# One-core Trainium2 kernel of four image stages: rows of q and k written by SBUF transfers, the neighbour mask as extra contraction rows, channel products on GpSimd, a new order of steps

## What is computed

```
stage 0: x1 = x + gap(x) . (w_conv x) . softmax_j(x^T x)
stage 1: q, k (16 rows each) and v (128 rows) are 1x1 projections of x1 with batch norm folded in
         x2 = x1 + gamma * v . softmax_j(q^T k)^T
stage 2: a, s (16 rows each) = relu(projection of x2)
         h_s = softmax over the 8 neighbours of a pixel of a^T s, applied to x2
         h_p = softmax over the 2 neighbouring channels of x2 x2^T, applied to x2
         x3 = (1 - gama) x2 + gama * elu(h_s + h_p)
stage 3: a 2-D Fourier transform of 16 projections of x3, gains by direction, inverse, added to x3
```

## Time and profile before

| | us |
|---|---|
| median of 3 runs (lowest, highest) | 290.1 (289.94, 290.49) |
| the profiled execution: its own time | 290.33 |
| the profiled execution: span in the trace | 288.5 |
| mean granted TensorE clock | 0.991 of full speed |
| instructions in the trace | 4440 |

### The profile page before, as it was taken

The page is one execution under the profiler, slowest core; times in us unless marked ns, Lnnn a source line. Parts: engine busy times, 40 slices in busy tenths (PEclk is TensorE's granted clock), DMA queues, the critical chain, the costliest instruction groups (busy, mean ns, idle before and its releaser), DMA issues.

```text
span 288.5 us, 4440 instructions
## 1 busy us (share of the span) xinstructions
PE 272.3 (94%) x1499; PEld 178.6 (62%) x1499; DVE 213.2 (74%) x325; ACT 186.2 (65%) x355; POOL 95.1 (33%) x102
## 2 busy tenths in 40 slices
PE   7999999999999899999999999799999799999994
PEld 3846555467677576747657464467867557765462
DVE  3865889789998786763489867799788775828383
ACT  0774676789997474766648776688748457674320
POOL 1045031505236878128004101354279814000000
PEclk9999999999999999999999999979999999999998
DMA  6951000000000000000000000000000000000015
GB/s 184 353 202 51 0 1 1 2 0 1 3 0 1 0 2 0 1 3 0 0 3 1 0 2 1 1 0 2 1 0 2 1 0 3 2 4 0 2 73 220
DMA packets 4520, 8.14 MB, mean 28 GB/s; under 512 B 1118, under 2 KB 2014, under 8 KB 4498
## 3 DMA queue, kind: packets, MB, share of 16 engines
q1 hardware_dynamic: 4498, 7.85, 7.8%
HBM read 5.68 MB, written 2.10 MB: 27 GB/s over the span
## 4 chain that ended last, share of the span: by engine, by line
PE 66%; DVE 10%; POOL 8%; ACT 8%; issue 3%; DMA 2%; SPq 1%; DVEq 0%; POOLq 0%; ACTq 0%
PE psum L360 64%; POOL e1h L1047 4%; ACT e L686 3%; DVE e1l L900 3%; DMA qs<-row 2%; ACT psum L677 2%; POOL ks L1040 1%; DVE nmax L884 1%; POOL qs L1037 1%; SPq L348 1%; DVE nmax L850 1%; ACT qs L669 1%; POOL regionb L1010 1%; ACT ks L670 1%; DVE x L860 1%
## 5 line engine op out<-in xcount | busy, mean ns | idle before, releaser
L1047 POOL CAST e1h<-e 128x1024 fp32r<-128x1024 f32 x32 | 42.6, 1333 | 34.7 <-ACT e L686 21.6
L900 DVE TENSOR_TENSOR e1l<-e,e1h 128x1024 fp32r<-128x1024 f32 x32 | 40.8, 1282 | 9.8 <-POOL e1h L1047 9.7
L686 ACT ACTIVATE e<-psum 128x1024 f32<-128x1024 f32 x32 | 32.8, 1025 | 20.6 <-DVE e1l L900 15.7
L850 DVE TENSOR_REDUCE nmax<-psum 128x1 f32<-128x1024 f32 x32 | 39.0, 1221 | 9.3 <-PE psum L360 8.7
L657 ACT ACTIVATE e<-psum,nmax 128x1024 f32<-128x1024 f32 x32 | 35.7, 1115 | 14.2 <-issue 9.6
L884 DVE TENSOR_REDUCE nmax<-psum 128x1 f32<-128x1024 f32 x32 | 38.0, 1217 | 3.9 <-PE psum L360 3.8
L677 ACT ACTIVATE psum<-psum,nmax 128x1024 f32<-128x1024 f32 x32 | 34.8, 1089 | 7.0 <-DVE nmax L884 6.3
L360 PE MATMUL psum<-e,v0n 128*64 128x512 f32 x128 | 31.0, 604 | 0.0
L360 PE MATMUL psum<-ks,qs 96*128 96x512 f32 (+2 forms) x96 | 30.1, 405 | 0.8 <-DVE ks L874 0.4
L360 PE MATMUL psum<-qs,ks 96*128 96x512 f32 (+2 forms) x96 | 28.9, 389 | 1.8 <-DMA qs<-row 1.3
L360 PE MATMUL psum<-xh 128*128 128x512 f32 x64 | 28.3, 442 | 0.6 <-DVE x L860 0.3
(11 more groups left out here) (175 smaller groups left out, 491.4 us busy)
## 6 DMA issues: line engine op xcount, KB each, us to landing
out<-xin SPq DMA_DIRECT2D x8, 256.0 KB, 2.1
xin<-in_x SPq DMA_DIRECT2D x3, 512.0 KB, 6.1
twist<-in_twist_in SPq DMA_DIRECT2D x1, 768.0 KB, 7.4
zz<-in_region_in SPq DMA_DIRECT2D x2, 360.0 KB, 3.5
xin<-in_x SPq DMA_DIRECT2D x2, 256.0 KB, 2.8
untwist<-in_untwist_in SPq DMA_DIRECT2D x1, 512.0 KB, 7.2
zz<-in_near_in SPq DMA_DIRECT2D x1, 288.0 KB, 4.4
rw<-in_rows_w SPq DMA_DIRECT2D x1, 256.0 KB, 2.7
```

The source lines that it names most:

```text
L686: inc(go(e1[:, E1_AT[b, i], :], t[:, :], ACT.Exp), "e1_ready", b)
L850: inc(vec.tensor_reduce(nmax0[z][:, i:i + 1], t[:, :], AX.X, ALU.max, negate=True), "nmax0_ready", b)
L900: inc(vec.tensor_tensor(e1l[:, EH_AT[b, i], :], e1[:, E1_AT[b, i], :], e1h[:, EH_AT[b, i], :].bitcast(F32), ALU.subtract), "e1l_ready", b)
L1047: done(gp.tensor_copy(e1h[:, EH_AT[b, i], :], e1[:, E1_AT[b, i], :]), "e1h_ready", b, i)
```

## The change

The parts of the diff that matter:

- **Rows.** qs and ks now have 80 rows and a margin of 32 pixels on either side. Groups are of 17 rows (16 and one for the shift). ACT writes the high parts of a projection in one activation of 128 x 512 to a buffer hi, DVE the rests in one to a buffer lo. SP then issues 12 transfers from SBUF to SBUF of 17 rows x 2 KB each: 8 from hi, 4 from lo. score and near wait for all 12. The steps qkdup and asdup of POOL are gone. SP has a written list of its own.
- **Bias.** For q and k the bias goes in with ACT and DVE; the pair of bias matmuls stays for a and s only.
- **Mask.** The neighbour mask is 29 further contraction rows of qs and ks, written once by four transfers of 29 rows x 4.3 KB after a cast on POOL. A window is one matmul with 80 rows and 192 columns. The mask's load stands behind those of images 2 and 3.
- **Channels.** chan's 8 matmuls and its mask become a product of neighbouring channels on POOL (cprod, 128 x 1016) and three sums (csum), then three fp32 matmuls of one or two columns. ecn is built from two columns by three DVE instructions in place of one.
- **Start.** POOL's memsets are others and more, and eight small copies clear the margins. The fold step has one transpose fewer.
- **Order.** All step lists are rewritten. On PE between a projection and the first matmul that reads its rows (or the shift rows that SP issues behind them) stand now: image 0 qk: gram, gap, gram, mix; image 1 qk: gram, shift1, val1; image 2 qk: gram, mix, chanT, gram, half of nearT, gram, gram; image 3 qk: shift1, val1, scoreT, scoreT; image 0 as: attH, scoreT, attL three times; image 1 as: xconv, chanT, x2T, half of nearT, mix; image 2 as: attL, scoreT, x2T, attH, scoreT, attL, attH, attL; image 3 as: shift2, chan, xturn, x2T, chanT, nearT.

```diff
 G = 32
+R = HID + 1
-KS3 = 3 * G
+KS3 = 3 * R
+MASKS = 29
+KS4 = KS3 + MASKS
...
-    "normv.0.0 masks.0.0 normv.0.1 normv.0.2 regions.0.0 split.1.0 split2.1.0 normv.0.3 normv.1.0 qkdup.0.0 "
-    "qkdup.0.1 normv.1.1 normv.1.2 normv.1.3 split.2.0 split2.2.0 qkdup.1.0 qkdup.1.1 e1h.0.0 e1h.0.1 e1h.0.2 "
-    "e1h.0.3 e1h.0.4 e1h.0.5 e1h.0.6 e1h.0.7 regions.0.1 e1h.1.0 e1h.1.1 e1h.1.2 normv.2.0 e1h.1.3 e1h.1.4 "
-    "asdup.0.0 e1h.1.5 asdup.0.1 e1h.1.6 e1h.1.7 normv.2.1 asdup.1.0 normv.2.2 asdup.1.1 split.3.0 xkeep.0.0 "
-    "normv.2.3 split2.3.0 qkdup.2.0 normv.3.0 qkdup.2.1 normv.3.1 normv.3.2 normv.3.3 xkeep.1.0 qkdup.3.0 "
-    "qkdup.3.1 e1h.2.0 e1h.2.1 e1h.2.2 e1h.2.3 e1h.2.4 e1h.2.5 e1h.2.6 e1h.2.7 e1h.3.0 e1h.3.1 e1h.3.2 xkeep.2.0 "
-    "e1h.3.3 e1h.3.4 asdup.2.0 asdup.2.1 e1h.3.5 e1h.3.6 e1h.3.7 asdup.3.0 asdup.3.1 xkeep.3.0")
-
-SP_STEPS = [(name, b, int(name == "shift2")) for name, b, i in DVE_STEPS if name in ("shift1", "shift2")]
+    "nears.0.0 normv.0.0 normv.0.1 split.1.0 split2.1.0 normv.0.2 normv.0.3 regions.0.0 normv.1.0 regions.0.1 "
+    "normv.1.1 normv.1.2 split.2.0 split2.2.0 normv.1.3 e1h.0.0 e1h.0.1 e1h.0.2 e1h.0.3 e1h.0.4 e1h.0.5 normv.2.0 "
+    "e1h.0.6 e1h.0.7 e1h.1.0 e1h.1.1 e1h.1.2 e1h.1.3 e1h.1.4 e1h.1.5 e1h.1.6 cprod.0.0 e1h.1.7 normv.2.1 csum.0.0 "
+    "split.3.0 split2.3.0 normv.2.2 cprod.1.0 normv.2.3 xkeep.1.0 xkeep.0.0 csum.1.0 normv.3.0 normv.3.1 "
+    "normv.3.2 normv.3.3 e1h.2.0 e1h.2.1 e1h.2.2 e1h.2.3 e1h.2.4 e1h.2.5 e1h.2.6 e1h.3.0 e1h.3.1 e1h.2.7 e1h.3.2 "
+    "e1h.3.3 e1h.3.4 e1h.3.5 e1h.3.6 e1h.3.7 cprod.2.0 csum.2.0 xkeep.3.0 cprod.3.0 csum.3.0 xkeep.2.0")
+
+SP_STEPS = steps(
+    "regin.0.0 nearin.0.0 regin.0.1 qkhi.0.0 qklo.0.0 qkhi.1.0 qklo.1.0 row1.0.0 row1.1.0 ashi.0.0 aslo.0.0 "
+    "row2.0.0 ashi.1.0 aslo.1.0 row2.1.0 qklo.2.0 qkhi.2.0 row1.2.0 qkhi.3.0 qklo.3.0 row1.3.0 ashi.2.0 aslo.2.0 "
+    "row2.2.0 ashi.3.0 aslo.3.0 row2.3.0")
...
+        qs = two("qs", [KS4, NW], F32R)
+        ks = two("ks", [KS4, NW], F32R)
+        hi = two("hi", [P, HALF], F32R)
+        lo = two("lo", [P, HALF], F32R)
...
+            sp.dma_start(near, near_in).then_inc(const_in, 16)
...
+            def rows(dst, at, src, k, z):
+
+                for h in range(2):
+                    o = h * 2 * G + k * G
+                    sp.dma_start(dst[z][at * R:(at + 1) * R, W + h * HALF:W + (h + 1) * HALF].bitcast(F32),
+                                 src[z][o:o + R, :].bitcast(F32)).then_inc(s["qk_in"][z], 16)
+
+            for name, b, i in SP_STEPS:
                 z = b % 2
-                wait(sp, "row_ready", b, n)
-                for k, to in ((0, HID), (1, 2 * G + HID)):
-                    sp.dma_start(qs[z][to:to + 1, :].bitcast(F32).rearrange("o (u p) -> o u p", p=P),
-                                 row[z][k * CH:(k + 1) * CH, :].bitcast(F32)).then_inc(s["shift_in"][z], 16)
+                if name in ("row1", "row2"):
+                    wait(sp, "row_ready", b, int(name == "row2"))
+                    for k, to in ((0, HID), (1, 2 * R + HID)):
+                        sp.dma_start(qs[z][to:to + 1, W:W + N].bitcast(F32).rearrange("o (u p) -> o u p", p=P),
+                                     row[z][k * CH:(k + 1) * CH, :].bitcast(F32)).then_inc(s["shift_in"][z], 16)
+                elif name == "nearin":
+                    wait(sp, "nearr_ready", 0)
+                    for k in range(2):
+                        for n, dst in enumerate((qs, ks)):
+                            sp.dma_start(dst[k][KS3:KS4, :].bitcast(F32),
+                                         nearr[n * 32:n * 32 + MASKS, :].bitcast(F32)).then_inc(near_sem, 16)
+                elif name == "regin":
+                    if i:
+                        wait(sp, "regions_ready", 0)
+                    sp.dma_start(region, region_in[:, i]).then_inc(region_sem, 16)
+                elif name in ("qkhi", "ashi"):
+                    wait(sp, "hi_ready", b, int(name == "ashi"))
+                    for dst, at, k in ((qs, 0, 0), (ks, 0, 1), (qs, 1, 0), (ks, 2, 1)):
+                        rows(dst, at, hi, k, z)
+                elif name in ("qklo", "aslo"):
+                    wait(sp, "low_ready", b, int(name == "aslo"))
+                    for dst, at, k in ((qs, 2, 0), (ks, 1, 1)):
+                        rows(dst, at, lo, k, z)
...
-                        mm(t[h * 2 * G:(h + 1) * 2 * G, 0:HALF], wT[:, k, 0:2 * G], src[:, h * HALF:(h + 1) * HALF],
-                           True, False, True)
-                    for h in range(2):
-                        last = mm(t[h * 2 * G:(h + 1) * 2 * G, 0:HALF], biasb[:, k, 0:2 * G], ones[:], False, True, True)
+                        last = mm(t[h * 2 * G:(h + 1) * 2 * G, 0:HALF], wT[:, k, 0:2 * G],
+                                  src[:, h * HALF:(h + 1) * HALF], True, k == QK, True)
+                    if k == AS:
+                        for h in range(2):
+                            last = mm(t[h * 2 * G:(h + 1) * 2 * G, 0:HALF], biasb[:, 0:2 * G], fill[0:3, :], False, True, True)
...
-                    wait(pe, "dup_ready", b, 3)
-                    wait(pe, "low_ready", b, 1)
+                    pe.wait_ge(s["qk_in"][z], ROWS_IN * (b // 2 * 2 + 1))
                     t = begin(step)
                     for h in range(2):
                         ho = slice(h * HALF, (h + 1) * HALF)
-                        last = mm(t[:, ho], qs[z][:, cols], ks[z][:, ho], True, True)
+                        last = mm(t[:, ho], qs[z][0:KS3, W + i * P:W + (i + 1) * P],
+                                  ks[z][0:KS3, W + h * HALF:W + (h + 1) * HALF], True, True)
...
-                    wait(pe, "x2T_ready", b)
-                    pe.wait_ge(s["masks_ready"][0], 3)
-                    t = begin(step)
-                    for u in range(CH):
-                        mm(t[:, 0:P], x2T[z][:, u, :], x2T[z][:, u, :], u == 0, False)
-                    end(step, mm(t[:, 0:P], identb[:], chainb[:], False, True))
+                    wait(pe, "cgram_ready", b, 3)
+                    pe.wait_ge(const_in, 16 * 2)
+                    t = begin(step)
+                    mm(t[:, 0:2], ident, edge[:], True, False, True)
+                    mm(t[:, 0:1], cgram[:, 0:P], one[:], False, False, True)
+                    end(step, mm(t[:, 1:2], cgram[:, 1:P + 1], one[:], False, True, True))
...
-                        kind = 1 if u == 0 else 2 if u == CH - 1 else 0
-                        lo, hi = max(u * P - W, 0), min((u + 1) * P + W, N)
                         w0 = (u % 4) * WPAD
-                        off = w0 + lo - (u * P - W)
-                        first = u % 2 == 0
-                        mm(t[:, w0:w0 + WIN], identb[:], nearb[:, kind, :], first, False, True)
-                        last = mm(t[:, off:off + hi - lo], lhs[:, u * P:(u + 1) * P], rhs[:, lo:hi],
-                                  False, not first, True)
+                        last = mm(t[:, w0:w0 + WIN], lhs[:, W + u * P:W + (u + 1) * P], rhs[:, u * P:u * P + WIN],
+                                  True, True)
                     end(step, last)
                 elif name == "join":
...
-                    first, func = (0, ACT.Copy) if name == "qkproj" else (2, ACT.Relu)
-                    t = take((name, b, 0))
-                    if first:
-                        wait(act, "e1_ready", b, CH - 1)
-                    q, k = slice(2 * i * G, (2 * i + 1) * G), slice((2 * i + 1) * G, (2 * i + 2) * G)
-                    inc(go(qs[z][0:G, hc], t[q, 0:HALF], func), "qhi_ready", b)
-                    inc(go(ks[z][2 * G:3 * G, hc], t[k, 0:HALF], func), "khi_ready", b)
+                    t = take(step)
+                    if name == "qkproj":
+                        inc(go(hi[z][:], t[:, 0:HALF], ACT.Identity, bias=bias[:, QK:QK + 1]), "hi_ready", b)
+                    else:
+                        inc(go(hi[z][:], t[:, 0:HALF], ACT.Relu), "hi_ready", b)
...
+                    n = int(name == "aslow")
+                    t = take((name[0:2] + "proj", b, 0))
+                    wait(dve, "hi_ready", b, n)
+                    by, op = (0.0, ALU.max) if n else (bias[:, QK:QK + 1], ALU.add)
+                    inc(vec.scalar_tensor_tensor(out=lo[z][:], in0=t[:, 0:HALF], scalar=by, in1=hi[z][:].bitcast(F32),
...
-                    inc(vec.tensor_scalar(ecn[z][:], ec[z][:], recc[z][:], None, ALU.mult), "ecn_ready", b)
+                    inc(vec.tensor_scalar(ecw[z][:], ec[z][:], recc[z][:], None, ALU.mult), "ecw_ready", b)
+                    wait(dve, "ecw_ready", b)
+                    inc(vec.tensor_scalar(ecu[z][:], above, ecw[z][:, 1:2], None, ALU.mult), "ecu_ready", b)
+                    wait(dve, "ecu_ready", b)
+                    inc(vec.scalar_tensor_tensor(out=ecn[z][:], in0=below, scalar=ecw[z][:, 0:1], in1=ecu[z][:],
...
+                elif name == "cprod":
+                    wait(pool, "x2T_ready", b)
                     settle()
```

(35 more changed lines are left out.)

179 lines of the change are left out of this document (87 added, 92 removed), and 145 rows, old and new, of tables (ACT_STEPS, DVE_STEPS, PE_TEXT).

## The result

The changed kernel takes **438.28 us** (median of 4 runs, 437.45 to 438.68); the kernel before took 290.3 beside it. The ratio is 1.509, 95% interval 1.506 to 1.513. The forecast was 408 with a range of 284 to 425: the direction and the main mechanism came, the size was 30 us short. A further run of a kernel can be some per cent longer at a lower granted clock; where the two runs of an experiment differ so, both times are given.

A forecast was written before the change was run, and what follows sets the result against it. TensorE's written order was taken as the bound: 290.3 us, -11.7 TensorE work, -8.8 absorbed idle, +124.3 pauses behind row transfers, +13.6 lower clock, giving 408 us, range 284 to 425.

The forecast's parts named there:

- TensorE bound by its order, eight joints: TensorE's written order sets the end; others matter at eight joints, two per image, from projection to first score or near.
- One engine, 1.49 us a transfer, 20.3 us a joint: Each 17-row transfer uses one DMA engine; twelve take 17.9 us, so TensorE stands 124.3 us in all; chance 0.55.
- the other reading: Row transfers use the smallest count of DMA engines with at most ceil(rows/16) rows each: 9 engines for 17 rows.
- rival (1): Rows spread over nine or more engines, SP's issuing limits: 7.7 us per joint, 296 us (294 to 314); chance 0.25.
- Rival (2): Spread and hidden: transfers issued in under 0.22 us, joints at most 4.8 us, 279 us, down to 270; chance 0.20.
- rival (3): At near blocks the mask saving is absent, the window alone being paced like the pair: +5.8 us on any case.
- eight times 13.6: TensorE restarts at the lower clock after each of eight pauses, losing 1.7 us each, 13.6 us in all.
- -11.7 TensorE work, -8.8 idle that the new pauses absorb: TensorE loses 11.7 us of work (near windows, channel product, bias pairs, transpose) and 8.8 us of existing idle.
- the sum's own 341 to 428: Range of the one-engine sum, from 0.8 us to 1.7 us per row transfer.
- GpSimd's 19 us "costed at nothing": GpSimd's channel products and sums, 4 x 4.75 = +19 us, do not set the end and cost nothing.
- the prediction's own sentence on the cover: Without TensorE's attention work beside them, GpSimd's products put up to 4.75 us ahead of join and delay queued e1h as much.
- the cover of 0.9: At the start, GpSimd's mask cast ends near 13.6 us, 0.9 us before the first v0n at 14.57.

The follow-up runs named there:

- rows18: The changed kernel with 18 rows per group in qs and ks instead of 17, nothing else: 368.6 us.
- rows32: The changed kernel with 32 rows per group in qs and ks instead of 17, and masks of 32 rows instead of 29: 340.8 us.
- hold_long: The changed kernel with 62 to 80 bf16 fill matmuls on constants put ahead of each joint's first matmul: 419.8 us.
- rows32_hold: rows32 with 18 to 32 bf16 fill matmuls on constants put ahead of each joint's first matmul: 324.0 us.
- pad17: The changed kernel with its 17-row transfers kept, but groups at every 32nd row with zeros between, so contractions take 96 rows instead of 51: 427.0 us.
- direct_old: The kernel before, its order and direct row writes kept, with mask as contraction rows, qkproj bias at eviction and channel products on GpSimd: 312.5 us.

## Why the prediction was right and wrong

**TensorE bound by its order, eight joints: right.** 126 us of its waits end in DMA qs or ks, in stands of 13.7 to 17.6 us.

**One engine, 1.49 us a transfer, 20.3 us a joint: right, and shown.** A set of 12 takes 17.5 to 17.9 us, up to 1.49 us a transfer; from the projection's end at 81.4 to the first score is 20.6 us at the joint above. TensorE's idle in the stands is 124.2 us against 124.3; from start to start they are 127.4. Joint by joint the start-to-start stands are within 1.0 us of the forecast but for image 2's qk, 15.2 us where 20.3 - 8.1 = 12.2 were taken: that the total of the idle agrees to 0.1 us is in part luck. rows18 rules out the other reading; so rival (1) was wrong in its premise, but its arithmetic (the joints at the pace of SP's issues) is what rows32 became, with a pitch of 0.63 for 0.48. Rival (2) fell with the issues of 0.6 us; rival (3) did not come: with waits left out and the ones at half clock halved, the 64 windows take 8.3 us from start to start where the 64 pairs took 14.1, -5.8 as forecast.

**The clock, "eight times 13.6" in all: the step that failed most.** 1.7 us a joint was read off one fall of the clock behind a small stand, where 3.5 us of work ran at half. Behind the stands of 14 to 18 us, 4 to 15 us of work ran so, 56.9 us in all, and 6.8 more from 400.8 us on: 63.7, half of it 31.8, less the 1.7 of before is 30.1, 16.5 more than forecast. hold_long and rows32_hold, where the fill keeps the clock up, show that this time is the clock's: 18 and 17 us came back. Why the clock stayed at half for 4 us behind one stand and 15 behind another is not shown.

**"-11.7 TensorE work, -8.8 idle that the new pauses absorb": the second.** Forecast, the rest was 281.2 - 11.7 - 8.8 = 260.7; measured, 271.9: 11.2 short. 9.1 to 9.6 of it is a cost that the sum had no term for: groups of 17 rows make a contraction of 51 rows in place of 96, and TensorE's steps around it are longer. pad17 and rows32 show it. The terms of the -11.7 came at the windows (5.8) and the channel step (1.14 us each for 1.12). The -8.8 did not come: outside the stands TensorE's idle fell from 10.9 to 9.1 us only. That the rest of rows32, 262.3, is so near 260.7 is in part luck: its idle there is 11.2 us, and its busy time, with the half-clock part halved, fell from 270.6 to 254.7, 4.2 more than the 11.7; where these 4.2 come from was not taken apart. The split closes: 3.1 + 16.5 + 11.2 = 30.8 for the 30 us missing.

**The range, "284 to 425".** Its upper part came from the sum's own 341 to 428, which let the time per transfer vary and nothing else. That time was right; the two terms that failed had no bounds of their own.

**GpSimd's 19 us "costed at nothing": right for the changed kernel, and only there.** In the changed kernel TensorE waits for no e1h and no cgram. That is not because all products ran inside stands: those of images 0 and 2 start at 170.2 and 357.4 us, between two stands, and behind a stand in which GpSimd had run empty (19.2 and 17.6 us idle before the e1h ahead of them). direct_old is the case without stands: the products put an e1h late, as the prediction's own sentence on the cover said, and the price was 24 us, 6 an image, above the 4.75 at most that it had for one.

**The start: wrong by little.** The mask load landed 2.5 us later than taken (its cast starts at 15.0, not 12.5), the cover of 0.9 was gone, and TensorE waited 0.8 us.
